# Down projection of a retention and FFN kernel: 17 products a tile, the last piece of h with both halves in one tile

## What is computed

```python
def fp4_linear(x, w):
    return jnp.einsum('bsk,nk->bsn', fp4_quant_dequant(x), fp4_quant_dequant(w))

gate = fp4_linear(x, w_gate)          # (2, 2048, 704)
y = fp4_linear(x, w_up)               # (2, 2048, 704)
h = silu(gate) * y
return fp4_linear(h, w_down)          # w_down (256, 704): the down projection

x = layernorm(x + retention(x, ...))
x = layernorm(x + ffn(x, ...))
```

## Time and profile before

| | before |
|---|---|
| median of 3 runs | 631.68 us (630.91 to 632.49) |
| the profiled execution | 630.28 us, of which the span of the profile is 628.3 us |
| TensorE matmul busy | 589.2 us (94%) |
| TensorE weight load busy | 499.6 us (80%) |
| VectorE busy | 552.6 us (88%) |
| ScalarE busy | 336.4 us (54%) |
| GpSimd busy | 231.9 us (37%) |
| mean granted TensorE clock | 0.978 |

### The profile page before, as it was taken

One profiled execution on the slowest core, in us unless ns is written; L12 is line 12 of the kernel. 1 busy time (PEld: TensorE's weight loads), 2 busy tenths in 40 slices (PEclk: granted clock), 3 DMA queues, 4 the chain that ended last, 5 costly groups with the idle time before them and its releaser, 6 DMA issues.

```text
span 628.3 us, 14715 instructions
## 1 busy us (share of the span) xinstructions
PE 589.2 (94%) x4304; PEld 499.6 (80%) x4304; DVE 552.6 (88%) x1439; ACT 336.4 (54%) x869; POOL 231.9 (37%) x263
## 2 busy tenths in 40 slices
PE   7999999999999999999999696969999999999975
PEld 3788888887878787888878575868999888888864
DVE  6667899999999999999998757879999999999996
ACT  3356575666667675756666553424444444444433
POOL 2111223442343244234421205445444545444530
PEclk9999999999999999999999989788999999999998
DMA  6510111011001101110110000000000000000001
GB/s 208 198 44 14 47 53 42 8 50 50 26 24 50 50 11 40 50 42 8 50 33 17 9 8 2 2 0 18 17 17 17 28 22 17 17 17 17 17 18 51
DMA packets 24951, 22.10 MB, mean 35 GB/s; under 512 B 2009, under 2 KB 21858, under 8 KB 24930
## 3 DMA queue, kind: packets, MB, share of 16 engines
q1 hardware_dynamic: 24114, 20.27, 10.6%
q10 hardware_dynamic: 816, 1.57, 0.7%
HBM read 17.63 MB, written 4.20 MB: 35 GB/s over the span
## 4 chain that ended last, share of the span: by engine, by line
DVE 23%; issue 12%; POOL 8%; PE 4%; ACT 2%; DVEq 1%; ACTq 0%; POOLq 0%
POOL shared L1166 4%; POOL shared L1171 3%; DVE shared L801 3%; DVE shared L806 2%; DVE h_amax L786 2%; DVE shared L1001 2%; DVE shared L997 1%; DVE win_lo L918 1%; ACT shared L541 1%; PE wide_banks L1195 1%; DVE stats L934 1%; DVE h_inv L797 1%; PE upd_y L1195 1%; DVE win_lo L921 1%; DVE h_scale L791 1%
## 5 line engine op out<-in xcount | busy, mean ns | idle before, releaser
L1171 POOL TENSOR_TENSOR shared<-shared,h_scale 128x704 f32<-128x704 bf16 x32 | 44.5, 1391 | 92.0 <-DVE shared L806 92.0
L1195 PE MATMUL wide_banks<-wgu_hi,xq_hi 128*128 128x512 f32 (+1 forms) x192 | 63.6, 413 | 9.4 <-DVE xq_lo L990 9.4
L444 ACT ACTIVATE shared<-opened,rstd 128x64 f32<-128x64 f32 x256 | 64.6, 335 | 11.6 <-DVE rstd L719 11.2
L1195 PE MATMUL wide_banks<-win_hi,x_hi 128*128 128x512 f32 x192 | 67.6, 433 | 1.9 <-DVE shared L629 1.9
L415 ACT ACTIVATE shared<-shared 128x704 bf16<-128x704 f32 x32 | 25.3, 792 | 82.0 <-POOL shared L1166 82.0
L1258 PEld LDWEIGHTS mixed<-shared 128*128 128x128 f32 x512 | 62.0, 192 | 2.8
L1166 POOL TENSOR_TENSOR shared<-shared,h_inv 128x704 f32<-128x704 f32 x32 | 44.6, 1393 | 49.8 <-DVE h_inv L797 49.8
L1258 PE MATMUL mixed<-shared 128*128 128x64 f32 x512 | 60.6, 271 | 0.0
L1195 PE MATMUL wide_banks<-win_hi,x_lo 128*128 128x512 f32 x192 | 60.4, 396 | 0.0
L1195 PE MATMUL wide_banks<-win_lo,x_hi 128*128 128x512 f32 x192 | 60.3, 395 | 0.0
L1195 PE MATMUL wide_banks<-wgu_hi,xq_lo 128*128 128x512 f32 (+1 forms) x192 | 58.2, 385 | 0.0
(11 more groups left out here) (153 smaller groups left out, 1499.9 us busy)
## 6 DMA issues: line engine op xcount, KB each, us to landing
xf<-in_x_feat SPq DMA_DIRECT2D x32, 128.0 KB, 2.2
tab<-in_tables SPq DMA_DIRECT2D x16, 256.0 KB, 2.7
xt<-in_x_tok SPq DMA_DIRECT2D x32, 128.0 KB, 2.1
out<-shared SPq DMA_DIRECT2D x32, 128.0 KB, 1.7
x<-in_w_in ACTq DMA_DIRECT2D x3, 512.0 KB, 5.3
w<-in_w_gu SPq DMA_DIRECT2D x1, 1408.0 KB, 7.5
w<-in_w_down SPq DMA_DIRECT2D x1, 704.0 KB, 8.7
wgu_lo<-pow_dram SPq DMA_DIRECT2D x1, 576.0 KB, 4.5
```

The lines of the kernel that those rows point to most:

```text
L444: last = act.activation(gated[:, b, cols], opened[:, b, cols], ACT.Copy, scale=rstd[:, b, 1 + k:2 + k])
L1171: pool.tensor_tensor(over_blocks(hq[:, b]), over_blocks(h_steps[:, b]), spread(h_fp4["scale"][:, b]), ALU.mult).then_inc(h_fp4["ready"], 1)
L1195: last = pe.matmul(dst, lhs, rhs, start=k == 0, stop=k == len(parts) - 1)
```

## The change

The sixth piece of h is laid out anew: its tile of h's high half keeps the high half of the 64 new columns in its rows 64 to 127, and gets their low half in its rows 0 to 63, in place of the repeated columns. The high half of the weights is copied into rows 0 to 63 as well, where zeros stood. One matmul of 128 rows then gives hi x hi + lo x hi for the last 64 columns, and hi x lo follows from a matmul of 64 rows (64 to 127). So a tile has 15 + 2 = 17 matmuls.

ScalarE writes the high half of all 768 columns in one operation across the two PSUM banks. VectorE's two operations stay two, but the first one takes 640 columns, and the second one the 128 columns of the last piece on 64 partitions, read from partitions 64 to 127 and written to partitions 0 to 63. In the setup ScalarE gets one operation more (64 partitions, 256 columns) and VectorE loses the two memsets.

```diff
+        turned_h = score.rearrange("p g t -> p (g t)")
+        TAIL = slice(P * (FC - 1), P * FC)
...
                 if old < BANK:
-                    act.activation(wdown_hi[F_OLD:P, c + 1], src[F_OLD:P, old:BANK], ACT.Copy).then_inc(w_hi_ready, 1)
+                    act.activation(wdown_hi[F_OLD:P, c + 1], src[F_OLD:P, old:BANK], ACT.Copy)
+                    act.activation(wdown_hi[0:F_OLD, c + 1], src[F_OLD:P, old:BANK], ACT.Copy).then_inc(w_hi_ready, 1)
...
             def split_h(n, b):
                 act.wait_ge(hT_done, n + 1)
                 need(act, z_done, n - 1)
-                act.activation(hT_hi[:, b, 0:BANK], score[:, 0], ACT.Copy)
-                act.activation(hT_hi[:, b, BANK:], score[:, 1, 0:FC * P - BANK], ACT.Copy).then_inc(hT_hi_ready, 1)
+                act.activation(hT_hi[:, b], turned_h[:, 0:FC * P], ACT.Copy).then_inc(hT_hi_ready, 1)
...
                 if old < BANK:
-                    dve.tensor_tensor(wdown_lo[F_OLD:P, c + 1], src[F_OLD:P, old:BANK], wdown_hi[F_OLD:P, c + 1].bitcast(F32), ALU.subtract)
-                    for part in (wdown_hi, wdown_lo):
-                        last = dve.memset(part[0:F_OLD, c + 1].bitcast(F32), 0.0)
+                    last = dve.tensor_tensor(wdown_lo[F_OLD:P, c + 1], src[F_OLD:P, old:BANK], wdown_hi[F_OLD:P, c + 1].bitcast(F32), ALU.subtract)
                 last.then_inc(w_lo_ready, 1)
...
             def split_h0(n, b):
                 dve.wait_ge(hT_hi_ready, n + 1)
                 need(dve, z_done, n - 1)
-                dve.tensor_tensor(hT_lo[:, b, 0:BANK], score[:, 0], hT_hi[:, b, 0:BANK].bitcast(F32), ALU.subtract)
+                body = slice(0, P * (FC - 1))
+                dve.tensor_tensor(hT_lo[:, b, body], turned_h[:, body], hT_hi[:, b, body].bitcast(F32), ALU.subtract)

             def split_h1(n, b):
-                dve.tensor_tensor(hT_lo[:, b, BANK:], score[:, 1, 0:FC * P - BANK], hT_hi[:, b, BANK:].bitcast(F32),
+
+                dve.tensor_tensor(hT_hi[0:F_OLD, b, TAIL], turned_h[F_OLD:P, TAIL], hT_hi[F_OLD:P, b, TAIL].bitcast(F32),
                                   ALU.subtract).then_inc(hT_lo_ready, 1)
...
                 accumulate(z_of(b), [(t[:, b, P * c:P * (c + 1)], w[:, c]) for t, w in
-                                     ((hT_hi, wdown_hi), (hT_hi, wdown_lo), (hT_lo, wdown_hi)) for c in range(FC)]).then_inc(z_done, 1)
+                                     ((hT_hi, wdown_hi), (hT_hi, wdown_lo), (hT_lo, wdown_hi)) for c in range(FC - 1)] +
+                           [(hT_hi[F_OLD:P, b, TAIL], wdown_lo[F_OLD:P, FC - 1]), (hT_hi[:, b, TAIL], wdown_hi[:, FC - 1])]).then_inc(z_done, 1)
```

## The result

| | before | after |
|---|---|---|
| median of the runs made side by side (11 each) | 631.94 us (630.62 to 634.09) | 634.12 us (633.40 to 636.78) |
| the profiled execution | 630.28 us, span 628.3 | 634.45 us, span 632.6 |
| TensorE matmul busy | 589.2 us | 593.3 us |
| VectorE busy | 552.6 us | 555.8 us |

The ratio of the times is 1.0038, with a 95% interval of 1.0023 to 1.0053. So one product less on each of 32 tiles comes with a kernel that is slower by 2.4 us (1.5 to 3.3).

The account below looks back on a forecast made before the run. The prediction took VectorE, with GpSimd between its steps, as the bound. Setup -0.37, steady FFN +2.6 and last tiles +0.6 gave +2.8 us on the median 631.68: 634.5 us, range 631.0 to 638.2.

Parts of the forecast that it names:

- What bounds: FFN: VectorE, with GpSimd's operations between its steps, sets 14.26 us a pair of tiles; TensorE needs about 13.8.
- TensorE's terms: FFN tile: one product less, -0.12 us; two changes of array shape, +0.40; 14.36 us a pair.
- VectorE's terms: Low-half split of h: lost overlap between operations, +0.21 us a pair to 14.47, +2.6 us in sum.
- Setup: Weight split: ScalarE's added operation +0.27 us, VectorE's dropped work -0.64; -0.37 in all, -0.26 if nothing overlaps.
- Last tiles: End of the FFN, engines in line: TensorE late by +0.04 + 0.28 + 0.28 = +0.6 us.
- TensorE's clock: Granted in full even with TensorE busy 14.88 of 20 us, so idle time should not move it; no term.
- Sum: Whole kernel: -0.37 + 2.6 + 0.6 = +2.8 us on the profiled 630.28; median 634.5 us.
- TensorE as the bound: Rival: array-shape changes above 0.23 us each make TensorE pass VectorE in the FFN; 638.3 us, chance 0.15.
- Everything hidden: Rival: VectorE's two split operations overlap as before, the pair stays 14.26 us; 631.8 us, chance 0.20.
- Product regained: Rival: TensorE bounds already and gets 0.12 us back on 28 tiles; 627.8 us, chance 0.06.
- Dear write: Rival: VectorE's 128-column operation, writing other partitions than it read, takes 0.28 us longer; 641 us, chance 0.09.

Follow-up runs that it names:

- neither: Changed kernel with the odd product on all 128 rows and VectorE's second low-half operation on partitions 0 to 63 (part left out); ratio 1.0003.
- mode_twice: Changed kernel with a second 64-row product among full ones (four array-shape changes a tile, part of a product left out); 643.02 us, ratio 1.0167.
- no_hold: Changed kernel with VectorE's second low-half operation reading and writing partitions 0 to 63 (part of the product left out), 64-row product kept; ratio 1.0004.
- low_rows: Changed kernel with h's last piece laid out the other way round: VectorE's second operation reads partitions 0 to 63, writes 64 to 127; ratio 1.0037.
- act_both: Changed kernel with full shapes and h's last piece at column 0; ScalarE crosses partitions in three operations, VectorE stays at partition 0; 632.38 us, ratio 1.0002.

## Why the prediction held, point by point

- **What bounds.** VectorE, with GpSimd: shown by the run *neither* (a product less and no new cost: no change) and by mode_twice (what it looks like when TensorE takes over). TensorE's need was a little too high in the text: its own step is 6.86, so 13.72 us a pair and not 13.8. And it was not seen that it enters the steady part late: in before it keeps its own step of 6.86 us up to 489 us, and the first wait that delays it, for GpSimd's xq, ends at 491 us. With 7.14 us a tile it waits only once in the stretch, hence its 160.00 busy us of 160. It still had 0.22 us a pair left. "VectorE has none" to spare was too strong: behind the split it had the 0.06 and 0.16 us above, in waits for GpSimd too short to stand in the earlier trace rows; the sum of the prediction did count them, as 0.98 and 1.09.
- **TensorE's terms.** -0.12 and +0.40 a tile: measured -0.12 and +0.38 to 0.41, in a shape that no row of before had. How they come was not as forecast: not 0.2 us before the 64-row product and 0.2 behind it, but 0.09 before, 0.19 behind, and 0.11 more before the next gate product.
- **VectorE's terms.** 1.14 us forecast from L919 to L999, 1.145 measured; a pair 14.47 forecast, 14.49 in the trace. The 0.02 us behind each held operation came as 0.01 and 0.03. The split into 0.815 and 0.28 came as 0.81 and 0.29. ScalarE's one operation, forecast at 0.82 us, takes 0.79 to 0.82. For the steady part 2.6 us were forecast; after less before is 2.65 between the first and the last split, and after less no_hold 3.0.
- **Setup.** -0.37 us forecast, -0.24 came: ScalarE's last full-height operation starts 0.17 us later than before (358.63 against 358.46, from the first layer), and `xq_lo` 0.07 us earlier (360.74 against 360.81). The step that failed is ScalarE's added operation: it costs 0.39 us, not 0.27; the prediction's own bound for no overlap, -0.26, is what came. The timeline of after shows why:

```profile
359.04 0.38 ACT L520 ACTIVATE win_hi<-wide_banks 64x256 fp32r<-64x256 f32 x1
359.43 0.38 ACT L521 ACTIVATE win_hi<-wide_banks 64x256 fp32r<-64x256 f32 x1
...
359.84 0.43 DVE L910 TENSOR_TENSOR win_lo<-wide_banks,win_hi 128x256 fp32r<-128x256 f32 x1 [0.77 <-ACT win_hi L521]
360.28 0.43 DVE L912 TENSOR_TENSOR win_lo<-wide_banks,win_hi 64x256 fp32r<-64x256 f32 x1
```

  L521 starts 0.39 us after L520, at that one's end. I had taken the overlap of 0.11 us from operations that all start at partition 0. Here none is left; L521 reads from 64 as L520 does, but writes from 0 after L520 wrote from 64. In low_rows, where the first two of these three operations start at partition 0, they do overlap, by 0.11 us.
- **Last tiles.** +0.6 forecast, +0.5 came, and it is TensorE's, as forecast: no_hold has it too (10.76 us from the last split to the end, as after, against 10.2 in before and in *neither*).
- **TensorE's clock.** The prediction had it unmoved by idle time, by a stretch with TensorE busy for 14.88 of 20 us. In the setup TensorE is busy for far less, and in both profiles the clock falls then or right behind it. The prediction has no term for it; the first split shows what single executions differ by ahead of the change's own loss, up to 3.2 us, more than the whole forecast. That no share of it is the change's is argued from the spread of these profiles, not shown by an experiment.
- **Sum.** +2.8 forecast; -0.2 + 2.65 + 0.5 = +2.95 by the trace, +2.2 to +2.4 by the medians. All three lie within the ratio's interval (1.5 to 3.3). The 0.55 to 0.75 us between the trace and the medians stay unexplained; single runs of one kernel differ by more.
- **The rivals.** TensorE as the bound: not the case, but near, since mode_twice shows the cost to be 0.19 to 0.20 a change, against the 0.23 from which it would have been (0.25 with the measured step of 6.86 us). Everything hidden: excluded, the overlap is gone in every tile. Product regained: excluded by the run *neither*, which has one product less at no cost and no gain. Dear write: excluded by the operation itself, which takes 0.29 us in after against 0.27 in no_hold.

## What to carry to other kernels

Before work is taken from the engine with the highest busy share, ask who waits for whom: here 0.12 us a tile taken from TensorE turned into its own waiting. And a busy share says nothing about an engine that entered the stretch late: TensorE was busy for all 160 us and had 0.22 us a pair to spare. A packing trick that moves data to other partitions is paid for on the engine that makes the move, by the overlap with its neighbours, so put it on an engine with room (act_both: nothing lost in the steady part, a little where the engines stand in line at the end), or keep its reads and writes at the start partition of what stands before and behind.

## What the runs showed of the hardware

An operation of VectorE that reads or writes from another start partition than the one before it (64 against 0) starts 0.01 to 0.02 us after that one's end, in place of 0.08 us ahead of it; the one that comes back to 0 starts 0.03 to 0.04 us after the end. So each costs about 0.1 us. ScalarE does likewise, which I had not expected. In act_both three of its operations follow each other, the third writing from partition 64:

```profile
508.46 0.71 ACT L539 ACTIVATE win_hi<-wide_banks 128x640 fp32r<-128x640 f32 x1
509.07 0.26 ACT L540 ACTIVATE win_hi<-wide_banks 64x128 fp32r<-64x128 f32 x1
509.34 0.27 ACT L541 ACTIVATE win_hi<-wide_banks 64x128 fp32r<-64x128 f32 x1
```

The second starts 0.10 us before the first ends, the third, which differs from the second only in the partitions that it writes, 0.01 us after the second's end; in the other tiles it is 0.00 to 0.02. And a matmul of 64 rows among full ones costs TensorE 0.38 to 0.41 us for going and coming back, more than three full products of 256 columns (0.12 us each).
